# The scan unit of a fused FFN / Mamba / FFN block: carry and scan cut 24 to 40 instead of 32 to 32, and the copies of u's turned pieces moved from ScalarE to VectorE

## The reference

```python
dA = exp(soft_clamp(dt[..., None] * A, -8, 8, 0.5))     # (b, t, E, N)
def step(h, inp):
    dA_t, dB_t, x_t, C_t, t = inp
    h = h * dA_t + dB_t * x_t[:, :, None]                # dB_t * x_t = B_t times (dt * xc) = B_t times u_t
    nrm = sqrt(sum(h * h, axis=(1, 2), keepdims=True))
    h = where(t % 10 == 0, h * minimum(20 / (nrm + 1e-8), 1), h)
    y = einsum('bdn,bn->bd', h, C_t) + D_param * x_t
    return h, y
```

## Time and profile before

| what | value |
|---|---|
| median of 3 runs | 1513.53 us (1511.62 to 1514.51) |
| profiled execution | 1517.25 us, of which the span of its instructions 1515.4 us |
| mean granted TensorE clock | 0.993 of full speed |
| busy share of the span | PE 95%, PEld 67%, DVE 83%, ACT 74%, POOL 62% |
| DVE scan, L1349 | 820 instructions, 710.5 us, 882 ns each |
| DVE carry, L1339 | 410 instructions, 137.1 us, 335 ns each |
| ACT copies of pieces, L956 and L976 | 60 and 60 of 128 x 256, 365 and 363 ns each |
| POOL norm, L1113, and weigh, L1124 | 410 each, 551 and 1447 ns each |

### The profile page before, as it was taken

How to read it: one execution, slowest core, us unless ns; L and a number is a source line. 1 busy time by engine, 2 the same in 40 slices (tenths; PEclk the granted TensorE clock), 3 DMA queues, 4 the chain that set the end, 5 groups by cost and what they waited for, 6 DMA issues and landing times.

```text
span 1515.4 us, 25723 instructions
## 1 busy us (share of the span) xinstructions
PE 1442.1 (95%) x7022; PEld 1019.0 (67%) x7022; DVE 1254.5 (83%) x2526; ACT 1120.2 (74%) x2618; POOL 942.7 (62%) x956
## 2 busy tenths in 40 slices
PE   6999999999789999999999999999999998999998
PEld 5555566655467777777777777777666666777776
DVE  7786666765489999999999999999999998788784
ACT  4455455657999999999999999999999964324243
POOL 0224332433189999999999999999999997400000
PEclk9999999999899999999999999999999999999999
DMA  8224446545666666666566656666444347465520
GB/s 272 84 91 137 160 130 171 172 144 173 191 208 175 179 156 184 165 174 178 155 166 181 189 153 170 175 171 172 117 108 118 93 128 220 122 212 175 168 69 28
DMA packets 232326, 236.30 MB, mean 156 GB/s; under 512 B 46296, under 2 KB 198040, under 8 KB 232184
## 3 DMA queue, kind: packets, MB, share of 16 engines
q1 hardware_dynamic: 231240, 233.34, 54.0%
q10 hardware_dynamic: 944, 1.31, 0.2%
HBM read 136.31 MB, written 98.56 MB: 155 GB/s over the span
## 4 chain that ended last, share of the span: by engine, by line
DVE 36%; POOL 14%; PE 12%; issue 6%; DVEq 1%; POOLq 1%; DMA 1%; ACT 0%; SPq 0%; ACTq 0%
DVE h L1349 23%; POOL rc L1113 13%; DVE banks L1339 9%; PE banks L1498 4%; PE banks L1519 3%; PE banks L1529 3%; DVE qs L1333 2%; PE banks L1173 1%; DVEq L1347 1%; DMA ub<-scratch_ub 1%; DVE q_ln_st L1775 1%; POOLq L1121 1%; DVE q_g L1684 1%; DVE q_x L1656 1%; PE banks L1539 0%
## 5 line engine op out<-in xcount | busy, mean ns | idle before, releaser
L1349 DVE TENSOR_TENSOR_SCAN h<-decay,banks 128x352 f32<-128x352 f32 x820 | 710.5, 882 | 57.3 <-DVE banks L1339 2.9
L1124 POOL TENSOR_TENSOR hc<-h,bc 128x640 f32<-128x640 f32 x410 | 593.1, 1447 | 0.0
L1173 PE MATMUL banks<-hc,w_ident 128*128 128x320 f32 (+1 forms) x1664 | 526.7, 440 | 0.1
L1242 ACT ACTIVATE tb<-dtc,a 128x320 f32<-128x320 f32 (+1 forms) x832 | 417.6, 557 | 4.8 <-DVE x L611 4.8
L1173 PEld LDWEIGHTS banks<-hc,w_ident 128*128 128x128 f32 x1664 | 285.0, 191 | 70.7 <-issue 0.8
L1264 ACT ACTIVATE decay<-tb 128x640 f32<-128x640 f32 x410 | 295.3, 724 | 0.0
L1113 POOL TENSOR_TENSOR rc<-qs,w_mhalf 128x1 f32<-128x1 f32 x410 | 225.8, 551 | 108.4 <-DVE qs L1333 108.4
L1159 PE MATMUL banks<-ub 128*128 128x176 f32 x1640 | 273.4, 289 | 2.4 <-DMA ub<-scratch_ub 2.4
L1152 PEld LDWEIGHTS banks<-sc_ss,sc_ones 128*128 128x128 f32 x820 | 123.6, 189 | 158.4 <-ACT sc_sq L1253 152.1
L1159 PEld LDWEIGHTS banks<-ub 128*128 128x128 f32 x1640 | 217.5, 193 | 2.6 <-DMA ub<-scratch_ub 2.5
L1152 PE MATMUL banks<-sc_ss,sc_ones 128*128 128x1 f32 x820 | 151.8, 254 | 37.8 <-ACT sc_sq L1253 19.1
(11 more groups left out here) (133 smaller groups left out, 1725.2 us busy)
## 6 DMA issues: line engine op xcount, KB each, us to landing
ub<-scratch_ub SPq DMA_DIRECT2D x410, 107.5 KB
bc<-scratch_blk SPq DMA_DIRECT2D x205, 160.0 KB, 3.5
scratch_ub<-turned SPq DMA_DIRECT2D x64, 512.0 KB, 3.5
scratch_ub<-spread SPq DMA_DIRECT2D x64, 176.0 KB, 2.4
scratch_xc<-xc SPq DMA_DIRECT2D x8, 1024.0 KB, 4.8
scratch_sg<-sg SPq DMA_DIRECT2D x8, 1024.0 KB, 5.9
piece<-scratch_u SPq DMA_DIRECT2D x32, 256.0 KB, 4.1
q_ys<-scratch_y SPq DMA_DIRECT2D x8, 1024.0 KB, 5.6
```

The costliest lines, as they stand in the source:

```text
L1124: pool.tensor_tensor(hc[:, pl % 2, :, at * S:(at + 1) * S] .rearrange("p (c b n) e -> p c b n e", c=KE, b=B)[:, :, b], state(m)[:, :, 0:S] ...
L1173: mm = pe.matmul(banks[:, y_bank(p), 0:KE * B * wide], w.ident[:], rhs, start=(n == 0), stop=(n == N - 1))
L1242: act.activation(tanh_rows(c, r), dtc[:, c % 2, k * B:(k + 1) * B, 0:blocks_of(c) * S].rearrange("p b (k e) -> p k b e", e=S), ACT.Tanh, s ...
L1349: dve.tensor_tensor_scan(state(m).rearrange("p r e -> p (r e)")[:, half], decay[:, m % DRING, half], psI[m % B][:, half], 0.0, ALU.mult, A ...
```

## The change

Three things change, all in the scan unit.

1. The 64 rows are cut into rows 0 to 23 and rows 24 to 63 (`FIRST_ROWS = 24`). `carry` becomes two instructions with a semaphore each, and each of the two scans waits for its own carry. The first scan has 264 elements on a partition and the second 440, where both had 352.
2. The copies of a piece's high and low part leave ScalarE's passes and stand in VectorE's pass, between `carry(m)` and `scan(m, 0)`: the high part in passes j + 3 and j + 4, the low part in passes j + 9 and j + 10. They keep their size, 128 x 256, and their waits (`ut_done`, `lo_done`, and the store of an older piece).
3. Waits follow: `norm` waits for both carry semaphores of the unit before, and `inputs` waits for h_ready[0] and h_ready[1] at its first and second matmul instead of its first and third. The high part of the two pieces that are made in the stage before stays with ScalarE.

```diff
-    inp_ready, carry_ready = sem("inp_ready"), sem("carry_ready")
+    inp_ready = sem("inp_ready")
+    carry_ready = [sem(f"carry_ready{x}") for x in range(2)]
...
+    FIRST_ROWS = 24
+    parts = [slice(0, FIRST_ROWS), slice(FIRST_ROWS, NCH)]
...
+    def copy_high(dve, k, src, e0, e1):
         if e0 == 0:
-            act.wait_ge(ut_done, k + 1)
-            if 1 <= k < 2 * B:
-                act.wait_ge(ut_out[(k - 1) % B], 32 * ((k - 1) // B + 1))
-            elif k >= 2 * B:
-                act.wait_ge(ut_out[k % B], 32 * (k // B))
-        act.activation(turned[place(k)][:, 0, e0:e1], src[:, e0:e1], ACT.Copy).then_inc(ut_hi, 1)
+            dve.wait_ge(ut_done, k + 1)
+            if k < 2 * B:
+                dve.wait_ge(ut_out[(k - 1) % B], 32 * ((k - 1) // B + 1))
+            else:
+                dve.wait_ge(ut_out[k % B], 32 * (k // B))
+        dve.tensor_copy(turned[place(k)][:, 0, e0:e1], src[:, e0:e1]).then_inc(ut_hi, 1)
...
-    def copy_low(act, k, src, e0, e1):
+    def copy_low(dve, k, src, e0, e1):
         if e0 == 0:
-            act.wait_ge(lo_done, k - B + 1)
-        act.activation(turned[place(k)][:, 1, e0:e1], src[:, e0:e1], ACT.Copy).then_inc(ut_lo, 1)
+            dve.wait_ge(lo_done, k - B + 1)
+        dve.tensor_copy(turned[place(k)][:, 1, e0:e1], src[:, e0:e1]).then_inc(ut_lo, 1)
...
             if m >= B:
-                pool.wait_ge(carry_ready, m - B + 1)
+                for x in range(2):
+                    pool.wait_ge(carry_ready[x], m - B + 1)
...
-                if m >= B and c % (KE // 2) == 0:
-                    pe.wait_ge(h_ready[c // (KE // 2)], m + 1)
+                if m >= B and c < 2:
+                    pe.wait_ge(h_ready[c], m + 1)
...
-            for x in range(2):
-                if m - 2 - x in pieces:
-                    high_piece(act, pieces[m - 2 - x], psT, x * E // 2, (x + 1) * E // 2)
-                if m - 8 - x in pieces:
-                    copy_low(act, pieces[m - 8 - x], psT, x * E // 2, (x + 1) * E // 2)
...
-            dve.tensor_scalar(inp(m)[:, :, 0], state(m - B)[:, :, S], rc[:, b:b + 1], None, ALU.mult
-                              ).then_inc(carry_ready, 1)
+            for x in range(2):
+                dve.tensor_scalar(inp(m)[:, parts[x], 0], state(m - B)[:, parts[x], S], rc[:, b:b + 1], None, ALU.mult
+                                  ).then_inc(carry_ready[x], 1)
...
-                dve.wait_ge(carry_ready, m + 1)
-            half = slice(x * HR * W, (x + 1) * HR * W)
-            dve.tensor_tensor_scan(state(m).rearrange("p r e -> p (r e)")[:, half], decay[:, m % DRING, half],
-                                   psI[m % B][:, half], 0.0, ALU.mult, ALU.add).then_inc(h_ready[x], 1)
+            dve.wait_ge(carry_ready[x], m + 1)
+            part = slice(parts[x].start * W, parts[x].stop * W)
+            dve.tensor_tensor_scan(state(m).rearrange("p r e -> p (r e)")[:, part], decay[:, m % DRING, part],
+                                   psI[m % B][:, part], 0.0, ALU.mult, ALU.add).then_inc(h_ready[x], 1)
...
         for m in range(UNITS):
             carry(m)
+            for x in range(2):
+                if m - 3 - x in pieces:
+                    copy_high(dve, pieces[m - 3 - x], psT, x * E // 2, (x + 1) * E // 2)
+                if m - 9 - x in pieces:
+                    copy_low(dve, pieces[m - 9 - x], psT, x * E // 2, (x + 1) * E // 2)
             scan(m, 0)
```

More of the change, by code:

```diff
@@ L524, in scalar @@
             if i in (6, 7):
-                scan.high_piece(act, i - 6, psD[:, 0], 0, E)
+                scan.high_piece(act, i - 6, psD[:, 0])
             if i >= 1:
@@ L947, in turn_piece, with high_piece @@
             mm.then_inc(ut_done, 1)
-    def high_piece(act, k, src, e0, e1):
-        if e0 == 0:
-            act.wait_ge(ut_done, k + 1)
-            if 1 <= k < 2 * B:
-                act.wait_ge(ut_out[(k - 1) % B], 32 * ((k - 1) // B + 1))
-            elif k >= 2 * B:
-                act.wait_ge(ut_out[k % B], 32 * (k // B))
-        act.activation(turned[place(k)][:, 0, e0:e1], src[:, e0:e1], ACT.Copy).then_inc(ut_hi, 1)
+    def high_piece(act, k, src):
+        act.wait_ge(ut_done, k + 1)
+        if k >= 1:
+            act.wait_ge(ut_out[(k - 1) % B], 32 * ((k - 1) // B + 1))
+        act.activation(turned[0][:, 0, :], src, ACT.Copy).then_inc(ut_hi, 1)
+    def copy_high(dve, k, src, e0, e1):
+        if e0 == 0:
+            dve.wait_ge(ut_done, k + 1)
[4 more added lines that the diff above has]
+        dve.tensor_copy(turned[place(k)][:, 0, e0:e1], src[:, e0:e1]).then_inc(ut_hi, 1)
     def low_piece(dve, k, src):
@@ L1299, in rows_at @@
             return c + 1, half, due
-        pieces = {piece_unit(k): k for k in range(B, PIECES)}
         for m in range(AHEAD):
@@ L1371, in vector @@
         clamp(1)
+        pieces = {piece_unit(k): k for k in range(B, PIECES)}
         for m in range(UNITS):
             carry(m)
+            for x in range(2):
[3 more added lines that the diff above has]
+                    copy_low(dve, pieces[m - 9 - x], psT, x * E // 2, (x + 1) * E // 2)
             scan(m, 0)
```

## The result

The changed kernel takes 1552.7 us (median of 4 runs, 1549.9 to 1554.2), the kernel before 1514.0 us beside it (1511.6 to 1516.1). The ratio is 1.0247, with a 95% interval of 1.0233 to 1.0262: slower by 35 to 40 us. The forecast was 1547 (1527 to 1571). The profiled execution has a span of 1550.9 us, 35.5 more than before. One of the four executions of e8 took 3286.0 us, for a reason that no run shows; its ratio leaves it out.

What follows compares the result with a forecast made beforehand. VectorE's list, tied with POOL's norm, was taken to bound the kernel. 28 pieces +36, first two +0.3 each, 93 later units -4, last 17 0: +33 us, 1550 profiled, median 1547, range 1527 to 1571.

Steps and rivals of the forecast that it cites:

- hidden loop: Scan unit: second scan, ACT's squares, PE's total, clamp; clamp no earlier than 0.94 us after the previous second scan's end.
- The plain unit: Scan unit without piece work: 2.09 us forecast for 2.13 before, a gain of 0.04.
- The waits: First copies of high and low part wait for PE's turn and last subtraction: units 0.66 and 0.75 us longer.
- T: The end of a unit's second scan, from which the prediction counts the next unit's times in us.
- copy without a wait: Second-half copy of high or low part on VectorE: unit 0.06 us longer than before, ending at T + 2.19.
- the carries' hold: Time both carries hold back VectorE's next instruction: 0.17 to 0.26 us, taken as 0.21.
- The 93 units behind the pieces: Some 93 scan units after the last piece, each 0.04 us shorter: -4 us.
- The range: 1527 to 1571 us; low end +0.67 a piece, high end +2.07 a piece.
- That the waits are hidden: Rival: turn and subtraction done before VectorE reaches the copies; faster, 1510 us; chance 0.05, mostly hidden within 0.2% 0.04.
- That the second carry stands behind the first: Rival: VectorE finishes one carry before the next, plain unit 2.26 us, time 1612 us; chance 0.04.
- PE as the bound: Rival: PE too full for shorter units, piece units stay at 2.13 us, time 1554 us; chance 0.15.
- The idle time: Profile sign: VectorE idle before waiting copies, 0.4 to 0.8 us each, 60 waits, some 30 to 40 us.
- +41 and 1555: Sum and time in us if each 256-element copy takes the skill's 0.39 us instead of 0.32.

Runs made afterwards that it cites:

- e8: The changed kernel with GpSimd's waits for the carries and for the scan's halves removed; 1551.2 us, ratio 1.0241.
- e9: The kernel before (one carry, copies on ScalarE) with GpSimd's waits for the carry and for the scan's halves removed; 1500.0 us, ratio 0.9899.
- e1: The changed kernel with TensorE's piece work (turning and subtraction) one pass earlier; 1524.3 us, ratio 1.0069.
- e3: The changed kernel with the split undone: one carry, scans of 32 and 32 rows, copies still on VectorE; 1553.3 us, ratio 1.0264.
- e2: The kernel before with only the split into 24 and 40 rows, copies staying on ScalarE; 1506.8 us, ratio 0.9956.
- e10: The changed kernel with 32 and 32 rows, TensorE's piece work one pass earlier, and no GpSimd waits for carries and scan halves; 1507.1 us, ratio 0.9943.
- e4: The kernel before with only the split, into 32 and 32 rows, copies on ScalarE; 1501.7 us, ratio 0.9926.
- e5: The kernel before with only the split, into 28 and 36 rows, copies on ScalarE; 1492.5 us, ratio 0.9860.
- e7: The kernel before with the split into 32 and 32 rows, copies on ScalarE, and no GpSimd waits for carries and scan halves; 1486.2 us, ratio 0.9818.

## Why the prediction was right

- **What bounds the kernel.** The prediction has VectorE's list and POOL's norm within a few hundredths of each other, and a hidden loop behind them. That was right but for the order: e9 shows that the norm's loop set 2.13.
- **The plain unit** was forecast at 2.09 and took 2.10, for the reason given: the clamp waits, because the longer second scan lies on the squares' loop (e8). That the two carries overlap was right: the second starts 0.15 after the first (a pair lasts 0.43, the second alone 0.28), and the first lasts 0.24. From first carry to first scan it took 0.37 of a forecast 0.36 to 0.43. The extra wait of POOL cost no time here, as forecast, but it was not free: from the clamp's end to the norm's start it went from 0.15 to 0.17, hidden behind the squares' loop.
- **The waits** came as described. The copies start at T + 0.71 (forecast 0.71) and T + 0.78 (0.80), and their units take 2.77 and 2.84 (2.79 and 2.88). Over a copy without a wait the forecast had 0.60 and 0.69, or 39 us for 30 pieces; e1 puts 28 us on them, as the copy without a wait was dearer.
- **The term that was mis-sized** is that copy: 2.19 forecast, 2.30 measured, twice a piece. The copy itself held VectorE 0.33 (0.32 forecast). It was the carries' hold, the time from the first carry to the next instruction: 0.33, against a bound of 0.17 to 0.26 and a choice of 0.21. A carry of 24 rows holds 0.15, where four instructions of 128 x 32 held 0.08 each. As an estimate from the holds of 24, 24 and 40, and 64 rows (0.15, 0.33, and 0.24 in e3), an instruction of this kind costs about 0.10 and 2.2 ns a row, so cutting it in two costs another 0.1.
- **How near the sum came is in part luck.** In the profiled executions, 28 pieces cost 39.2 us and not 36. Against a mean unit of 2.147 before, the copies without a wait were 5.6 us dearer than forecast, the units that wait 3.2 cheaper, and the six units without a copy 0.8 dearer. The 93 units behind the pieces were forecast at -4 and gave -2.2; the first two pieces, forecast at +0.6, cost nothing; the last 17 units, forecast at 0, took 1.4 less. Together that is +33 forecast and +35.5 measured: part of the errors cancel. The rest of the gap between 1547 and 1552.7 comes from the 3.7 by which the profiled execution before lay above its median, and which the one after did not repeat.
- **The range.** Its high end does not come out as it is written: counted with four copies a piece, as the low end is, the terms make +2.23 a piece and an end of 1576. The result lies inside either way.
- **Rivals.** That the waits are hidden fell in the trace. That the second carry stands behind the first fell too, though a carry does cost more than the small instructions that spoke against it. PE as the bound fell: the units with subtraction take 2.10 in the changed kernel and in e2 (651.12 is followed by second scans at 653.22, 655.33, 657.43 and 659.53).
- **The idle time** that the profile puts before a waiting copy is 0.37 and 0.43, some 23 us over 57 recorded waits, and not the 30 to 40 that I named: it counts from the end of the carries (0.43 long), while the copy without a wait starts 0.33 after their start. The cost of a wait is read against the unit without one: 0.47 and 0.54.

On the copy's price, the Trainium skill (VectorE: DVE Perf Modes, section The TRN2 errata) gives 0.39 us as an estimate; the trace has 0.42 from start to end and 0.33 until the next instruction starts, and only the second counts in a full list. The +41 and 1555 that the prediction works out from that figure lie nearer to the measured time than its own sum, but not for their reason: the copy held 0.33, and the carries in front of it were what cost more. The same page's rule that the next instruction waits for an empty pipe (section The DRAIN you can't avoid) does not hold in these rows: the copy at 650.13 starts while the carries are running, until 650.23. That section adds that a next instruction which is not held starts earlier, and points to the section Two Vector instructions with no wait between them; with that the trace agrees.

Two things were not tried: copies at another place of VectorE's pass, and cuts between 28 and 32 with fewer waits.

## What to carry to other kernels

When an instruction moves to another engine's list, ask when that list reaches it and when its input is ready, in the same clock; a wait that cost nothing on an engine that came late becomes the whole engine's wait on one that comes early. A hole in the busiest engine is not free room: here the split nearly closed the hole, so that the copies that were to fill it paid most of their time (a unit 0.27 longer in e10, for a copy that holds 0.33). When a unit of work is bound by several loops, list each loop's sum before the cut is moved, and look for waits that another wait already implies: taking those away and cutting in the middle gave 1486 us, 1.8% under the kernel before.

## What the runs showed of the hardware

- Waits that had long been met still cost time on GpSimd where they stand in the list with one that is late. From the clamp's end to the norm's start it took, in the median of plain units, 0.17 to 0.18 us with three waits in front of the norm (the changed kernel, e2, e4, e5), 0.15 with two (the kernel before) and 0.08 with one (e7, e8, e9, which also lack the waits of the weighing behind it). That it is the number of waits and not which they are was not tried apart.
- A VectorE carry with rows 44 bytes apart, out to PSUM, holds the next instruction 0.15 us for 24 elements and lasts 0.24, where a 128 x 32 instruction at another place of this kernel held 0.08. Whether the operation, the stride or the output's place does it was not tried.
